# Two attention layers in one pipeline of sixteen batches, with norm factors per batch on GpSimd

## What is computed

```python
def _L2_xattn_ref(queries, context, wq, bq, wk, bk, wv, bv, wo, bo):
    ...
    q = queries @ wq.T + bq
    k = context @ wk.T + bk
    v = context @ wv.T + bv
    attn = jnp.einsum('bhnd,bhsd->bhns', q, k) * scale
    attn = jax.nn.softmax(attn, axis=-1)
    out = jnp.einsum('bhns,bhsd->bhnd', attn, v)
    return out @ wo.T + bo

def _L2_ffn_ref(x, Wq, bq, Wk, bk, Wv, bv, Wp, bp, Wr, br, Ws, bs, temperature, query_embedding):
    ...
    q_norm = q / jnp.linalg.norm(q, axis=-1, keepdims=True)
    q_scaled = (q_norm + query_embedding[None]) * jax.nn.softplus(temperature)[None]
    attn = jnp.einsum('bhqd,bhkd->bhqk', q_scaled, k) / math.sqrt(hd)
    ...
    gates = jax.nn.softmax(h @ Wr.T + br, axis=-1)
    _, idx = jax.lax.top_k(gates, ROUTED_HEADS)
    ...
    sw = jax.nn.softmax(h @ Ws.T + bs, axis=-1)
```

## Time and profile before

| | us |
|---|---|
| median of 3 runs (2131.7 to 2133.6) | 2133.0 |
| the profiled execution: its time | 2134.6 |
| the profiled execution: its span | 2132.9 |
| a2 | 237.3 |
| f2 | 304.1 |

### The profile page before, as it was taken

How to read it: one execution, slowest core, us unless ns; L and a number is a source line. 1 busy time by engine, 2 the same in 40 slices (tenths; PEclk the granted TensorE clock), 3 DMA queues, 4 the chain that set the end, 5 groups by cost and what they waited for, 6 DMA issues and landing times. The chain is left out here.

```text
span 2132.9 us, 33593 instructions
## 1 busy us (share of the span) xinstructions
PE 1620.8 (76%) x12250; PEld 1242.0 (58%) x12251; DVE 997.8 (47%) x2191; ACT 675.5 (32%) x1408; POOL 516.5 (24%) x583
## 2 busy tenths in 40 slices
PE   4898783640878636993589846888789999999976
PEld 3665662530656435883466524555468888888766
DVE  2675362224455541112266645676535544555542
ACT  1464341110455411110256522443432222222111
POOL 2110053014343220003433044441022222222110
PEclk8898696775999857997699975887989999999986
DMA  4230543223644237881556214343020000000001
GB/s 132 69 79 18 208 190 102 84 74 114 160 117 111 55 128 267 310 320 51 153 127 145 41 40 107 95 99 91 2 95 7 6 6 2 6 6 1 2 6 40
DMA packets 89424, 195.47 MB, mean 92 GB/s; under 512 B 13536, under 2 KB 62176, under 8 KB 80704
## 3 DMA queue, kind: packets, MB, share of 16 engines
q1 hardware_dynamic: 76352, 173.07, 28.2%
q0 software_dynamic: 4608, 12.59, 1.8%
q10 hardware_dynamic: 8320, 7.87, 1.1%
HBM read 136.47 MB, written 57.02 MB: 91 GB/s over the span
## 5 line engine op out<-in xcount | busy, mean ns | idle before, releaser
L806 DVE TENSOR_REDUCE a_sb_mx<-a_mx 128x2 f32<-128x512 f32 x256 | 164.9, 687 | 97.5 <-PE a_mx L634 97.2
L1161 DVE RECIPROCAL a_sb_rden<-a_ot 128x256 f32<-128x256 f32 x64 | 112.1, 1752 | 146.6 <-PE a_ot L1047 146.5
L558 ACT ACTIVATE a_sb_probs<-a_ex 128x512 f32<-128x512 f32 x256 | 139.2, 598 | 104.9 <-PE a_ex L655 104.5
L230 PE MATMUL a_gp<-g_ident,a_sb_xn 128*128 128x128 f32 x128 | 25.2, 330 | 163.8 <-POOL a_sb_xn L206 79.6
L230 PEld LDWEIGHTS a_gp<-g_ident,a_sb_xn 128*128 128x128 f32 x128 | 16.8, 165 | 167.8 <-DMA a_sb_bo<-a_bo 72.0
L806 DVE TENSOR_REDUCE f_sb_mx<-f_mx 128x2 f32<-128x512 f32 x128 | 82.3, 686 | 39.1 <-PE f_mx L634 38.7
L558 ACT ACTIVATE f_sb_probs<-f_ex 128x512 f32<-128x512 f32 x128 | 69.5, 597 | 76.2 <-PE f_ex L655 76.0
L990 ACT ACTIVATE a_sb_probs<-a_sc 128x512 f32<-128x512 f32 x64 | 38.2, 597 | 166.8 <-PE a_sc L1035 110.5
L959 POOL TENSOR_SCALAR_AFFINE_SELECT a_sb_probs<-a_sb_probs 128x256 f32<-128x256 f32 x128 | 49.0, 406 | 164.0 <-ACT a_sb_probs L991 163.9
L655 PE MATMUL a_ex<-a_sb_QP,a_sb_KP 49*128 49x256 f32 x512 | 68.3, 344 | 23.7 <-ACT a_sb_probs L558 21.1
L2466 PE MATMUL f_hb<-f_sb_xsT,f_sb_wb 128*128 128x128 f32 x640 | 75.9, 281 | 11.3 <-ACT f_sb_xsT L2419 11.3
(11 more groups left out here) (429 smaller groups left out, 3961.9 us busy)
## 6 DMA issues: line engine op xcount, KB each, us to landing
f_sb_wb<-f_w SPq DMA_DIRECT2D x20, 2052.0 KB, 11.3
a_sb_kvT<-ctxT SPq DMA_DIRECT2D x32, 256.0 KB, 3.4
...
```

The costliest lines, as they stand in the source:

```text
L558: act.activation(probs[:, group % 3, 2 * (u % 2) + par], EX[par][:], ACT.Exp, scale=scale)\
L806: dve.tensor_reduce(mx[:, :, column(2 * u + par)], MX[par][:], AX.X, ALU.max, negate=True)\
L1161: dve.reciprocal(rden[:, n], OT[n][:, 1, :])
```

## The change

`attention16` takes a list of layers. a0 is a call with one, a2 and f2 are one call with two: batches 0 to 7 are those of a2, 8 to 15 those of f2, in steps -1 to 20. Each layer has its own weights and biases, all loaded at the start. Batch b of f2 works on x of batch b - 8 when a2 has ended it, so its norm factors can't be formed for all tiles at once: `batch_norm_factors` forms them for the two tiles of a batch on GpSimd ahead of normalising, with an inverse root of a guess by integer arithmetic and three refinements.

The router's own work is divided otherwise. DVE biases q, ACT squares (place 2), DVE sums (place 3), GpSimd forms the roots as above and multiplies by the softplus of the temperature (place 4), DVE scales behind v (place 6). The embedding, scaled at the start, is added by ACT as a bias when it splits the transposed q. The copies of the negated maxima in f2 are ACT's. The gate takes its eight largest logits on DVE before the Exp, which becomes six of ACT that sum as well. The two banks of maxima become one tensor that DVE reduces in one operation, in a0 too.

```diff
+def batch_norm_factors(eng, g, b, ln):
+
+    at = slice(b * TT, (b + 1) * TT)
+    st = lambda i: g.stats[:, at, i]
+    eng.tensor_tensor(ln[:, 0, :], st(1), st(4), ALU.add)
+    eng.tensor_tensor(ln[:, 1, :], st(1), st(4), ALU.subtract)
+    eng.tensor_tensor(ln[:, 2, :], st(2), st(5), ALU.add)
+    eng.drain()
+    eng.tensor_scalar(g.mean[:, at], ln[:, 0, :], 0.5, None, ALU.mult)
+    eng.tensor_tensor(ln[:, 1, :], ln[:, 1, :], ln[:, 1, :], ALU.mult)
+    eng.tensor_scalar(ln[:, 2, :], ln[:, 2, :], 1.0 / D, EPS, ALU.mult, ALU.add)
+    eng.drain()
+    eng.tensor_scalar(ln[:, 1, :], ln[:, 1, :], 0.25, None, ALU.mult)
+    eng.drain()
+    eng.tensor_tensor(ln[:, 3, :], ln[:, 1, :], ln[:, 2, :], ALU.add)
+    eng.drain()
+    root_guess(eng, g.rstd[:, at], ln[:, 3, :])
+    for _ in range(3):
+        root(eng, g.rstd[:, at], ln[:, 3, :], g.rstd[:, at], ln[:, 4, :])
...
-ROUTED_EXTRAS = {0: [("neg1", 3), ("xT", 0), ("weigh3", 4), ("y", 5)], 1: [("q", 0), ("square", 0), ("out1", 4)],
-                 2: [("weigh0", 3), ("T0", 4), ("T1", 4)], 3: [("k", 0)], 4: [("neg0", 2), ("weigh1", 3), ("aT", 4)],
-                 5: [("scale", 0), ("gate", 4), ("v", 0), ("out0", 3), ("norm", -1)], 6: [("weigh2", 3), ("gexp", 4)],
+ROUTED_EXTRAS = {0: [("neg1", 3), ("xT", 0), ("weigh3", 4), ("y", 5)], 1: [("q", 0), ("out1", 4)],
+                 2: [("square", 0), ("weigh0", 3), ("T0", 4), ("T1", 4)], 3: [("k", 0), ("sums", 0)],
+                 4: [("neg0", 2), ("weigh1", 3), ("aT", 4), ("roots", 0)],
+                 5: [("gate", 4), ("out0", 3), ("norm", -1)], 6: [("weigh2", 3), ("gexp", 4), ("v", 0), ("scale", 0)],
                  7: [("qT", 0), ("factor", 4)]}
...
+def head_steps(routed):
+
+    n_b = B * len(routed)
+    of_layer = lambda b, which: 0 <= b < n_b and routed[b // B] == which
+    steps, moves = [], []
+    for s in range(-1, n_b + LOOKAHEAD):
         step = []
         for n in range(H // 2):
             step += [(f"score{n}", s - 3), (f"max{n}", s - 2)]
-            step += [(what, s - part) for what, part in extras.get(n, [])]
-        steps.append([(what, b) for what, b in step if 0 <= b < B])
-    return steps
+            for which, extras in ((True, ROUTED_EXTRAS), (False, HEAD_EXTRAS)):
+                step += [(what, s - part) for what, part in extras.get(n, []) if of_layer(s - part, which)]
+        steps.append([(what, b) for what, b in step if 0 <= b < n_b])
+        moves += [(what, s - part) for what, part, kinds in MOVES
+                  if 0 <= s - part < n_b and routed[(s - part) // B] in kinds]
...
+                        if b >= B:
+                            pool.wait_ge(stats_ready, b - B + 1)
+                            batch_norm_factors(pool, g, b % B, ln)
...
-                    elif what == "square":
-                        pool.wait_ge(q_sums, b + 1)
-                        pool.tensor_tensor(qn[:, 2], qn[:, 0], half[:], ALU.pow).then_inc(q_roots, 1)
+                    elif what == "roots":
+                        r = b - of(b).first
+                        pool.wait_ge(q_summed, r + 1)
+                        if r == 0:
+                            pool.wait_ge(centre, 1)
+                        else:
+                            pool.wait_ge(q_scaled, r)
+                        root_guess(pool, qn[:, 3], qn[:, 0])
+                        for _ in range(3):
+                            root(pool, qn[:, 3], qn[:, 0], qn[:, 3], qn[:, 1])
+                        by_token = lambda a: a.rearrange("p (t h) -> p t h", t=TT)
+                        pool.tensor_tensor(by_token(qn[:, 2]), by_token(qn[:, 3]),
+                                           spq[:, 0:H].rearrange("p (a h) -> p a h", a=1).broadcast_to([P, TT, H]),
+                                           ALU.mult).then_inc(q_rooted, 1)
...
+                    elif what == "square":
+                        act.wait_ge(q_biased, b - of(b).first + 1)
+                        act.activation(qsq[:], qtm[:], ACT.Square).then_inc(q_squared, 1)
...
+                        split_rows("qT", b, qf, qs, q_split, q_out, qe)
...
-                        act.wait_ge(gate_in, b + 1)
-                        act.activation(le[:, :, 0:H + 1], lg[:, :, 0:H + 1], ACT.Exp).then_inc(gate_exp, 1)
+                        act.wait_ge(gate_in, b - of(b).first + 1)
+                        for t in range(TT):
+                            act.activation(le[:, t, 0:H - 1], lg[:, t, 0:H - 1], ACT.Exp, bias=neg_top[:, t, 0:1],
+                                           accum_out=sums[:, t, 0:1])
+                            act.activation(le[:, t, H + 1:H + 4], top[:, t, 0:3], ACT.Exp, bias=neg_top[:, t, 0:1],
+                                           accum_out=sums[:, t, 1:2])
+                            op = act.activation(le[:, t, H - 1:H + 1], lg[:, t, H - 1:H + 1], ACT.Exp,
+                                                bias=neg_top[:, t, 1:2], accum_out=sums[:, t, 2:3])
+                        op.then_inc(gate_exp, 1)
...
-                dve.tensor_tensor(qsq[:], qtm[:], qtm[:], ALU.mult)
-                dve.drain()
+                dve.sem_inc(q_biased, 1)
+
+            def sum_q(b):
+                r = b - of(b).first
+                dve.wait_ge(q_squared, r + 1)
+                at_least(dve, q_rooted, r)
                 dve.tensor_reduce(qn[:, 0].rearrange("p (a h) -> p a h", h=8), per_head(qsq[:]), AX.X, ALU.add)\
-                   .then_inc(q_sums, 1)
+                   .then_inc(q_summed, 1)
...
-                dve.wait_ge(q_roots, b + 1)
-                root(dve, qn[:, 2], qn[:, 0], qn[:, 2], qn[:, 1])
-                by_token = lambda a: a.rearrange("p (t h) -> p t h", t=TT)
-                dve.tensor_tensor(by_token(qn[:, 2]), by_token(qn[:, 2]),
-                                  spq[:].rearrange("p (a h) -> p a h", a=1).broadcast_to([P, TT, H]), ALU.mult)
-                dve.drain()
+                dve.wait_ge(q_rooted, b - of(b).first + 1)
                 rows = qtm[:].rearrange("p t (c r h) -> p (t c) r h", c=KD, r=16)
                 dve.tensor_tensor(rows, rows, qn[:, 2].rearrange("p (c a h) -> p c a h", a=1, h=8)
-                                  .broadcast_to([P, TT * KD, 16, 8]), ALU.mult)
-                dve.drain()
-                dve.tensor_tensor(qtm[:], qtm[:], over_tokens(qe), ALU.add).then_inc(q_scaled, 1)
...
-                        for par in range(2):
-                            dve.wait_ge(mx_full[par], 8 * b + u + 1)
-                            dve.tensor_reduce(mx[:, :, column(2 * u + par)], MX[par][:], AX.X, ALU.max, negate=True)\
-                               .then_inc(mx_read[par], 1)
-                    elif what.startswith("neg"):
+                        dve.wait_ge(mx_full, 2 * (8 * b + u + 1))
+                        pair = mx[:].rearrange("p t (i g h) -> p g t i h", i=2, g=2)[:, :, :, u // 4, u % 4]
+                        dve.tensor_reduce(pair, MX[:], AX.X, ALU.max, negate=True).then_inc(mx_read, 1)
...
-                attention16(nc, g, s, w, bias=True)
+                layers = [(sub(io, n + "_"), n == "f2") for n in ("a2", "f2") if n in stages]
+                attention16(nc, g, s, layers)
...
-                attention16(nc, g, s, w, bias=True, kv_from_x=True, router=True)
...
```

296 lines of the change are left out of this document (159 added, 137 removed).

## The result

| | before | after |
|---|---|---|
| median, us | 2133.3 (2131.7 to 2134.4, 4 runs) | 2112.2 (2104.8 to 2116.1, 4 runs) |
| ratio | | 0.990, 95% interval 0.988 to 0.992 |
| span of the profiled execution | 2132.9 | 2114.4 |
| a2 and f2 | 541.5 | 516.6 |

A forecast was written before the change was run, and what follows sets the result against it. The prediction took a ring of small GpSimd operations with PE as the bound: 166.9 + 8 x 26.5 + 72 = 450.9 us against 541.5, so 90.6 us off 2133.0 gives 2042, range 2012 to 2090.

The forecast's parts named there:

- Part 1, the seam: Merging a2 and f2: sixteen batches in 22 steps, not two times 14; 166.9 us to step 8, added loads costed at nothing.
- Part 2, the PE bound: Steps 8 to 15: PE's work alone needs 24 us a step, including 0.7 us waiting for the scaled query.
- More than 1 us there: Sign of a wrong forecast: DVE's or ACT's queue holds PE at qT for more than 1 us.
- Part 3, the ring: GpSimd's chains and PE's transposition of xn form a loop, taken as the bound: 26.5 us a step, chance 0.50.
- R + N: GpSimd's time per batch for the roots (R, 4.6 us) and the norm factors (N, 5.2 us).
- the 13.4 us from xn's transposition to k's rest: Ring term read in a2: from xn's transposition to the split of k with GpSimd's subtraction done, 13.4 us.
- 0.8 us for the clock: Added to the ring's 25.7 us a step because PE won't hold full clock throughout, giving 26.5.
- "2 to 3 us" of waiting for xn: Sign of the ring: PE's longest wait in steps 9 to 15 is for GpSimd's normalising, 2 to 3 us each.
- the steps 8 to 14 alike: All these steps hold the ring; steps 8 to 12 differing much from 13 to 15 would show the forecast wrong.
- only the seam pays: Rival: merged steps stay at f2's 30.8 us, 56 us saved, 2077 us; chance 0.23 for steps of 30 to 33.
- Part 4, pairs: Paired maxima reduction on DVE, 1.23 us: nothing on the path, here and in a0; bounds -1 to +3 us.
- Part 5, the emptying: End of the merged stage: 72 us, bounds 70 and 76, with 2.7 us taken back from shorter gate chains.

The follow-up runs named there:

- e1: The changed kernel with the moved maxima's load put ahead of the KP loads in SP's order, as before the change: 2083.7 us, 0.975 of before.
- e4: The kernel before with only the KP loads put ahead of the moved maxima's load in SP's order: 2157.1 us, 1.012 of before.
- e3: The changed kernel with the edits of both e1 and e2: 2035.4 us, 0.953 of before.
- e6: The changed kernel with the next batch's norm factors formed at place 0 of the step, its normalising left at place 5: 2061.0 us, 0.964 of before.
- e9: The kernel of e6 with e1's order on SP's queue as well: 2031.6 us, 0.952 of before.
- e2: The changed kernel with norm factors and normalising moved from place 5 to 2, ahead of k's rest and the roots on GpSimd: 2063.2 us, 0.968 of before.
- e8: The kernel before with only the paired maxima taken over, one reduction in place of two: 2123.3 us, 0.994 of before.
- e13: The kernel of e9 with the router's copies of the negated maxima moved back from ACT to DVE: 2040.7 us, 0.956 of before.

## Why the prediction missed, step by step

**Part 1, the seam.** "166.9 us up to step 8 (as now)" is the first step that failed: 188.6. I looked at the loads that the change adds at the start and not at the table of moves, whose two exchanged entries I should have followed to the next wait on each. At SP's pace the maxima stand 1.8 us later (1124.71 to 1126.51) and behind four transfers, and land some 7 us after their issue. Undoing it takes 24.0 us off (e1), and doing it alone makes the loss in the kernel before (e4). The start itself was costed rightly: the first batches run at the same distances, e3's first part is 165.9.

**Part 2, the PE bound.** Right, 24 us forecast and 23.6 in e3 and e6. DVE and ACT are as expected, 16.8 and 16.3 us in a ring of after (forecast: falling towards 14.1, and 13.4 + 3). The wait for the scaled query is 0.8 in the step of after shown above (0.7 forecast; 1.4 at most), and 1.4 on average in e3. More than 1 us there was named as a sign of being wrong, so this came out larger than forecast, though it isn't what holds the steps of after.

**Part 3, the ring.** The mechanism was right and named as the bound, its size was not: 29.8 us a step against 26.5. Two terms of the ring were too small. The first is R + N, 12.7 us measured for 9.8. The operations took what the line said (0.24 for 32 columns where it gave 0.25, 0.20 for two where it gave 0.18), but starts lie 0.38 and 0.34 apart: one that waits for the one before costs 0.14 more and not the 0.08 taken from DVE.

The second is the 13.4 us from xn's transposition to k's rest, read in a2. In after it is 12.9 us in the steps 8 and 9, where PE doesn't wait for xn, and 13.8 to 17.6 in the steps 10 to 15; the mean of all eight is 15.1. The kernels with the ring open tell why. In e9, with the clock at 1.00, it is 12.6 to 12.9 us in the steps 8 to 12 and 14.6 to 14.7 in the steps 13 to 15. There PE multiplies by wo for the router's finished batch right behind the transposition, 1.99 us, which in a2's steps comes last. Rows of step 14 of e9, on PE and on POOL:

```profile
1308.53 0.66 PE L252 MATMUL a_gp<-g_ident,a_sb_xn 128*128 128x128 f32 x4 [0.34 <-ACT a_sb_qs L598]
...
1310.12 1.99 PE L676 MATMUL a_gp<-a_sb_wo,a_sb_oT 128*128 128x256 f32 x8
```

```profile
1321.93 1.27 POOL L540 TENSOR_TENSOR a_sb_ks<-a_sb_kf,a_sb_ks 128x512 fp32r<-128x512 f32 x1 [5.62 <-ACT a_sb_ks L598]
```

The rest is the clock, 0.81 to 0.90 in that stretch of after. The trace of before had a row that warned of it: in f2's step 6 the transposition stands at 1411.94 and k's rest ends 20.0 us later, of which up to 5.5 are the power ahead of it:

```profile
1425.17 5.45 POOL L498 TENSOR_TENSOR f_sb_qn<-f_sb_qn,f_sb_half 128x32 f32<-128x32 f32 x1 [12.72 <-DVE f_sb_qn L719]
1430.68 1.27 POOL L483 TENSOR_TENSOR f_sb_ks<-f_sb_kf,f_sb_ks 128x512 fp32r<-128x512 f32 x1
```

The two errors feed each other. A ring that makes PE wait 6 us in a step went with a clock of 0.82, and at that clock the PE part of the ring is longer. I had added 0.8 us for the clock. "2 to 3 us" of waiting for xn were 5.0 to 6.6. And the ring didn't hold the steps 8 to 14 alike: the steps 8 to 12 are 28.3 us on average and 13 to 15 32.2, which the prediction named as a sign of being wrong.

The rival "only the seam pays" has the step (30.8) nearest to the measured 29.8, but not for its reason: with the ring open the low clock went (e2, e3).

**Part 4, pairs.** The reduction takes 1.22 us as forecast:

```profile
L881 DVE TENSOR_REDUCE a_sb_mx<-a_mx 128x4 f32<-128x1024 f32 x192 | 234.8, 1223 | 166.1 <-PE a_mx L719 163.6
```

"Nothing on the path" is wrong: e8 shows 9 to 12 us less in all, outside the bounds of -1 to +3, and shorter steady steps in f2. The sentence "PE already waited for both halves" left out that it did wait, 3.3 us in a step. In a2's full steps (21.2 us before, 21.0 in e8) nearly nothing shows, and a0 took 213.9 us against 219.2 and 215.7, within what executions differ by.

**Part 5, the emptying.** 72 forecast, 84.1 measured from the same mark. The reading under it was wrong: from PE's first scores of its step 8 on, f2 took 82.4 us to empty and not 74.7, so the gate and its chains made 12.0 us against a2's 70.4 and not 4.3, and the stretch at the start of the last part (7.7 us before, 5.8 after) is in no term. One execution of e2 had 73.0 at a clock of 0.93, so behind that mark the work was sized rightly and the clock wasn't: DVE's work did shrink (42.6 to 37.7 us), and PE's busy time grew from 56.1 to 64.3 at the same count. What in the router's new work brings the low clock is open. ACT's copies aren't it (e13). The gate's new form with its six Exp and the embedding added by ACT weren't tried alone.

**The sum.** The errors are 22 us in the first part, 26 in the eight steps, 6 in the stretch without a term and 12 in the emptying. With f2's 7.7 us put in, the same working would have given 2050, still 62 us short. The range allowed a step of 32.5, but only with the first part and the emptying near what they were; it took in the unknowns of one term and none of the others.
